# 16-bit slot marks, running sums by a scan, expert tiles spread from step 42 to step 244 with some of them halved, and the last merge divided between VectorE and GpSimd

## What is computed

```python
x = L0_attn_x
xn = _layernorm(x, axis=-1)
x = x + attention(xn, W_q, W_k, W_v, W_o) + experts(xn, Wg, gamma, beta, W1, b1, W2, b2)

# attention: 16 heads of 8 features, rotary embedding, full softmax over 1024 keys
scores = einsum('bhqd,bhkd->bhqk', Q, K) / sqrt(8)
out = einsum('bhqk,bhkd->bhqd', softmax(scores), V) ... @ W_o.T

# experts: 8 experts, each token goes to its best 2
w, idx = top_k(xf @ Wg, 2);  w = softmax(w)
normed = layernorm(xf) * gamma[e] + beta[e]
h = relu(normed @ W1[e] + b1[e])              # 128 -> 512
out = h @ W2[e] + b2[e] + xf                  # 512 -> 128
y = sum over the two chosen experts of w * out
```

## Time and profile before

| | |
|---|---|
| runs (3) | 587.09, 589.49, 590.52 us; median 589.49 |
| profiled execution | 589.15 us, span 587.2 us |
| PE busy | 541.0 us (92%) |
| ACT busy | 501.4 us (85%) |
| DVE busy | 300.9 us (51%) |
| POOL busy | 246.0 us (42%) |
| chain that ended last | PE 63%, ACT 21%, DVE 8% |

### The profile page before, as it was taken

The page is one execution under the profiler, slowest core; times in us unless marked ns, Lnnn a source line. Parts: engine busy times, 40 slices in busy tenths (PEclk is TensorE's granted clock), DMA queues, the critical chain, the costliest instruction groups (busy, mean ns, idle before and its releaser), DMA issues.

```text
span 587.2 us, 12446 instructions
## 1 busy us (share of the span) xinstructions
PE 541.0 (92%) x4620; PEld 246.0 (42%) x4620; DVE 300.9 (51%) x1002; ACT 501.4 (85%) x552; POOL 246.0 (42%) x303
## 2 busy tenths in 40 slices
PE   8899988878999999999899999999989999999783
PEld 6323312222455554445345555434534555554111
DVE  4975789965434344463344433555433444343672
ACT  2699999989898788898888888899899888888992
POOL 4299900078646444556223444365521444322000
PEclk9999999999999999999999999999999999999996
DMA  7144320051435545324443464433433455460821
GB/s 257 29 138 123 113 62 11 1 181 49 159 108 165 185 149 162 99 75 149 136 133 105 163 211 153 141 100 100 160 98 114 154 176 188 142 188 30 315 81 39
DMA packets 44657, 75.47 MB, mean 129 GB/s; under 512 B 7585, under 2 KB 17873, under 8 KB 44081
## 3 DMA queue, kind: packets, MB, share of 16 engines
q1 hardware_dynamic: 39232, 63.71, 33.9%
q0 software_dynamic: 4544, 9.32, 5.2%
q10 hardware_dynamic: 816, 1.61, 0.7%
HBM read 33.88 MB, written 8.85 MB: 73 GB/s over the span
## 4 chain that ended last, share of the span: by engine, by line
PE 63%; ACT 21%; DVE 8%; issue 3%; DMA 2%; POOL 1%; SPq 1%; ACTq 1%; another core or an unknown queue 0%; POOLq 0%; DVEq 0%
PE acc L696 29%; ACT ring L921 20%; PE sc L661 11%; PE aside_bank L740 9%; PE sc L754 8%; PE aside_bank L768 2%; DMA sin<-rope_sin 2%; DVE xn L1228 2%; PE aside_bank L572 1%; PE sc L729 1%; DVE xn L1230 1%; DVE xn L1233 1%; PE aside_bank L588 1%; DVE blocks L1089 1%; SPq L332 1%
## 5 line engine op out<-in xcount | busy, mean ns | idle before, releaser
L921 ACT ACTIVATE ring<-sc 128x1024 f32<-128x1024 f32 x512 | 488.0, 1040 | 59.9 <-PE sc L661 55.9
L696 PE MATMUL acc<-ring,v 128*9 128x512 f32 x2048 | 250.9, 595 | 18.3 <-ACT ring L921 11.8
L513 POOL DMA_INDIRECT work<-normed,token x71 | 71.3, 1004 | 235.1 <-DVE work L1290 181.5
L661 PE MATMUL sc<-qs,ks 32*128 32x512 f16 x1024 | 101.4, 384 | 16.2 <-ACT ring L921 14.1
L1296 DVE TENSOR_SCALAR work<-aside_bank,xn 128x128 f32<-128x128 f32 x216 | 60.8, 345 | 107.1 <-PE aside_bank L740 105.8
L661 PEld LDWEIGHTS sc<-qs,ks 32*128 32x128 f16 x1024 | 26.2, 91 | 177.5 <-ACT ring L921 150.6
L696 PEld LDWEIGHTS acc<-ring,v 128*9 128x9 f32 x2048 | 39.9, 89 | 117.0 <-issue 76.5
L523 POOL DMA_INDIRECT token_out<-work,token x71 | 69.8, 983 | 37.6 <-issue 19.2
L740 PE MATMUL aside_bank<-work,xn 128*128 128x128 f32 x432 | 62.6, 288 | 0.0
L740 PEld LDWEIGHTS aside_bank<-work,xn 128*128 128x128 f32 x432 | 52.3, 191 | 12.2 <-issue 12.2
L754 PE MATMUL sc<-xn,work 128*128 128x128 f32 x432 | 57.2, 275 | 0.0
(11 more groups left out here) (194 smaller groups left out, 416.4 us busy)
## 6 DMA issues: line engine op xcount, KB each, us to landing
xn<-w_rest SPq DMA_DIRECT2D x54, 323.0 KB
xn<-L_ffn_W SPq DMA_DIRECT2D x54, 256.0 KB
w_last<-w_rest SPq DMA_DIRECT2D x17, 323.0 KB
w_last<-L_ffn_W SPq DMA_DIRECT2D x17, 256.0 KB
qs<-hl SPq DMA_DIRECT2D x60, 64.0 KB
ks<-hl SPq DMA_DIRECT2D x60, 64.0 KB
x<-L_attn_x SPq DMA_DIRECT2D x4, 512.0 KB, 8.2
w_rest<-L_ffn_W SPq DMA_DIRECT2D x8, 256.0 KB, 4.0
```

Of the source, the lines that this page charges most:

```text
L513: pool.indirect_dma_start(out=xt[t % TILE_BUFFERS], out_offset=None, in_=xh_d[:, :], in_offset=bass.IndirectOffsetOnAxis(ap=token[:, 0, t: ...
L661: last = nc.tensor.matmul(dst, ks[r:r + 32, kb * P:(kb + 1) * P], qs[r:r + 32, at], start=True, stop=not slow)
L696: last = nc.tensor.matmul(acc[32 * j:32 * j + VW, :], v9[:, b, kb, 4 * g + j, :], ring[:, (2 * n + j // 2) % UNITS, j % 2, :], start=(kb = ...
L921: nc.scalar.activation(ring[:, (2 * n + u) % UNITS, :, :], sc[HOME[2 * n + u]][:, :].rearrange("p (h c) -> p h c", h=2), ACT.Exp, scale=SC ...
```

## The change

1. `mark` compares in 16 bit. Its two index tables are made once by POOL (three copies behind the store of the normed rows), the slots' halves are bf16, and the tables have the 8 columns of a group innermost. `invert` now reads place and name with a step of 8 elements.
2. `place` gets its running sums from two scans instead of chains of shifted additions; `ranks` multiplies by the negated complement of the old triangle.
3. The marks move from steps 32 to 44 to steps 26 to 34, the inversions to 29 to 36, `tokens` from 47 to 36, `owners` to 37, `gates` to 43, the four projections of batch 1 to 38, 40, 46 and 50.
4. The tiles start at step 42 and end at step 242. `ONE_AT` says where layer one of a tile stands, `TWO_AT` where layer two and the turning stand. 58 steps have both. 13 steps have layer one only and 13 others layer two and the turning only, and step 242 the last layer two. `NORM_AT` moves by two steps, and the norm and bound checks share a step with a half.
5. The expert rows are loaded back from step 244 and merged at steps 248 to 251. DVE merges 6 of a batch's 8 rows of tiles (12 instructions instead of 16), POOL the other 2 (4 products and 2 sums a batch). `add_out` of the last batch and the stores wait for both.
6. On PE, `weigh(255)` and `project_out(3, 1)` move into the innermost blocks (`finish`). The last `take_sums`, `divide` and `add_out` of DVE stay behind the blocks.

```diff
-ROUTE_AT, RANKS_AT, SLOTS_AT, OWNER_AT, GATES_AT = 21, 24, 24, 29, 39
-INVERT_AT = {n: g for g, n in enumerate((35, 37, 38, 40, 43, 44, 46, 47))}
-MARK_AT = {n: g for g, n in enumerate((32, 33, 35, 37, 40, 41, 43, 44))}
-TOKENS_AT = 47
-PLAIN_AT = {n: (1, r) for r, n in enumerate((28, 49, 50, 54))}
+ROUTE_AT, RANKS_AT, SLOTS_AT, OWNER_AT, GATES_AT = 21, 24, 24, 37, 43
+INVERT_AT = {n: g for g, n in enumerate(range(29, 29 + GROUPS))}
+MARK_AT = {n: g for g, n in enumerate((26, 27, 29, 30, 31, 32, 33, 34))}
+TOKENS_AT = 36
+PLAIN_AT = {n: (1, r) for r, n in enumerate((38, 40, 46, 50))}
...
-FFN_FROM = 52
-TILE_AT = {n: k for k, n in enumerate([n for n in range(FFN_FROM, STEPS, 2) if n not in TAKEN][:SLOT_TILES + 1])}
+FFN_FROM, FFN_TO = 42, 244
+SMALL = [n for at in (NORM_AT, FLAG_AT) for n in at]
+FREE = [n for n in PAIRS if n not in PLAIN_AT and n not in PROJECT_AT]
+HALVED = [(FREE[FREE.index(n) - 1], n) for n in SMALL]
...
+for n in FREE:
+    if n not in SPLIT_PAIRS or SPLIT_PAIRS.index(n) % 2 == 0:
+        ONE_AT[n] = len(ONE_AT)
+    if n not in SPLIT_PAIRS or SPLIT_PAIRS.index(n) % 2:
+        TWO_AT[n] = len(TWO_AT)
...
-MERGE_AT = {LOAD_AT + 4 + 3 * b: b for b in range(B)}
+LOAD_AT = FFN_TO
+MERGE_AT = {LOAD_AT + 4 + b: b for b in range(B)}
+DVE_TILES = 6
...
+            pool.wait_ge(xh_out, 16 * B)
+            nc.gpsimd.tensor_copy(all_places, iota_p.unsqueeze(2).to_broadcast([P, P, GROUP])).then_inc(indices_ok, 1)
...
+            for b in range(B):
+                pool.wait_ge(y_home[b], 16)
+                y = y_in[b].rearrange("p (t k d) -> p t k d", t=TB, k=2)
+                for k in range(2):
+                    for u in range(DVE_TILES, TB):
+                        t = TB * b + u
+                        last = nc.gpsimd.tensor_scalar(y[:, u, k, :], y[:, u, k, :], small[:, 2 + k, t:t + 1], None, ALU.mult)
+                after(last)
+                rest = x[:, TB * b + DVE_TILES:TB * (b + 1), :]
+                after(nc.gpsimd.tensor_tensor(rest, rest, y[:, DVE_TILES:TB, 0, :], ALU.add))
+                last = nc.gpsimd.tensor_tensor(rest, rest, y[:, DVE_TILES:TB, 1, :], ALU.add)
+                last.then_inc(merged_pool, 1)
...
-                    last = nc.tensor.matmul(bank[0][:, 0:2 * SLOT_TILES], place_mark[g % 2][:, i, :],
-                                            named[g % 2][:, i, :, :].rearrange("p v c -> p (v c)"),
+                    last = nc.tensor.matmul(bank[0][:, 0:2 * SLOT_TILES], place_mark[g % 2][:, :, i],
+                                            named[g % 2][:, :, :, i].rearrange("p v c -> p (v c)"),
...
-                        if n - 2 in TILE_AT:
-                            pe.wait_ge(tile_taken, TILE_AT[n - 2] + 1)
+                        if n - 2 in TWO_AT:
+                            pe.wait_ge(tile_taken, TWO_AT[n - 2] + 1)
...
+            def finish():
+                weigh(STEPS - 1)
+                project_out(B - 1, 1)
...
+                link(nc.vector.tensor_tensor_scan(upto, not_first, totals, 0.0, ALU.mult, ALU.add))
...
+                link(nc.vector.tensor_tensor(tile_mark[k], all_tiles, slot_hl[:, 0, js].unsqueeze(1).to_broadcast(of_tiles),
+                                             ALU.is_equal))
+                nc.vector.tensor_tensor(place_mark[k], all_places,
+                                        slot_hl[:, 1, js].unsqueeze(1).to_broadcast([P, P, GROUP]), ALU.is_equal)
+                nc.vector.tensor_scalar(named[k][:, 0, :, :], tile_mark[k], row_name, None, ALU.mult)
+                nc.vector.tensor_tensor(named[k][:, 1, :, :], tile_mark[k],
+                                        pick_16[:, js].unsqueeze(1).to_broadcast(of_tiles), ALU.mult).then_inc(mark_ok, 1)
...
                 if b == B - 1:
                     v.wait_ge(merged, B)
+                    v.wait_ge(merged_pool, B)
...
-                    for u in range(TB):
+                    for u in range(DVE_TILES):
```

More of the change, by code:

```diff
@@ L98 @@
-SINE_AT = {n + 1 if n != 28 else 48: piece for n, piece in PLAIN_AT.items()}
+FFN_FROM, FFN_TO = 42, 244
+PAIRS = range(FFN_FROM, FFN_TO, 2)
+SMALL = [n for at in (NORM_AT, FLAG_AT) for n in at]
+FREE = [n for n in PAIRS if n not in PLAIN_AT and n not in PROJECT_AT]
+HALVED = [(FREE[FREE.index(n) - 1], n) for n in SMALL]
+SPLIT_PAIRS = [n for pair in HALVED for n in pair]
+MORE = len(FREE) - len(SMALL) - (SLOT_TILES + 1)
+assert len(set(SPLIT_PAIRS)) == 2 * len(SMALL) and MORE >= 0
+for m in range(MORE):
+    at = FREE.index(PER_BATCH + 8 + (STEPS - PER_BATCH) // (MORE + 1) * m)
+    while FREE[at] in SPLIT_PAIRS or FREE[at + 1] in SPLIT_PAIRS:
+        at += 1
+    SPLIT_PAIRS += [FREE[at], FREE[at + 1]]
@@ L99 @@
+ONE_AT, TWO_AT = {}, {}
+for n in FREE:
[3 more added lines that the diff above has]
+        TWO_AT[n] = len(TWO_AT)
+del ONE_AT[max(ONE_AT)]
+TWO_STEP = {k: n for n, k in TWO_AT.items()}
+assert len(ONE_AT) == SLOT_TILES and len(TWO_AT) == SLOT_TILES + 1
+SINE_AT = {n + 1: piece for n, piece in PLAIN_AT.items()}
 SQUARE_AT = {n + 5: piece for n, piece in PLAIN_AT.items() if piece[0] > 1}
-SQUARE_AT.update({n: (1, r) for r, n in enumerate((53, 55, 56, 57))})
@@ L101 @@
-SPLIT_ROUND = {piece: 3 if n < FFN_FROM + 4 else 5 + min(k for k, step in TILE_STEP.items() if step > n)
+SQUARE_AT.update({n: (1, r) for r, n in enumerate((43, 45, 50, 54))})
+SPLIT_ROUND = {piece: 3 if n < FFN_FROM else 5 + max(k for k, step in TWO_STEP.items() if step < n)
                for n, piece in SINE_AT.items()}
-WEIGHTS_AT = {n: k + 3 for n, k in TILE_AT.items() if k >= 1 and k + 3 < SLOT_TILES}
-LOAD_AT = TILE_STEP[SLOT_TILES] + 2
-MERGE_AT = {LOAD_AT + 4 + 3 * b: b for b in range(B)}
+WEIGHTS_AT = {n: k + 3 for n, k in TWO_AT.items() if k >= 1 and k + 3 < SLOT_TILES}
@@ L151, in score_homes @@
             order = [2] + order
-        before = n - 2 if n - 2 in TILE_AT else None
+        before = n - 2 if n - 2 in TWO_AT else None
         for u in range(2):
@@ L671, in maxima @@
                 wait(pe, e_ok, 2 * PER_QUAD * q)
-                wait(pe, tile_taken, len([n for n in TILE_AT if n < PER_QUAD * q]))
+                wait(pe, tile_taken, len([n for n in TWO_AT if n < PER_QUAD * q]))
                 pe.wait_ge(m_wide[b], 2 * (base + 1))
@@ L791, in aside @@
                     first_tile()
-                if n in TILE_AT:
-                    tile(TILE_AT[n], n)
+                if n in ONE_AT:
+                    layer_one(ONE_AT[n])
+                if n in TWO_AT:
+                    layer_two_and_turn(TWO_AT[n], n)
                 if n in NORM_AT:
@@ L854, in batches @@
                         batches(b + 1, following)
+                    else:
+                        finish()
                 with pe.Else():
```

114 lines of the change are left out of this document (49 added, 65 removed).

## The result

The changed kernel takes 607.24 us (median of 4 runs, 606.68 to 607.46); the kernel before took 588.29 us beside it (4 runs, 586.73 to 590.52). The ratio is 1.032, with an interval of 1.028 to 1.036: slower by 3.2%. The forecast was 593.2, with a range of 583.5 to 600, so it was wrong in size. The profiled execution took 607.02 us, of which 605.2 are the span: 18.0 more than the span before.

The account below looks back on a forecast made before the run. Pairs of steps without a tile follow ACT (3.7 us); pairs with one wait over a score home (4.58). Plus 0.3 early, minus 1 tiles, plus 4.6 end is plus 3.9 on 589.15: 593.05, taken as 593.2, range 583.5 to 600.

Parts of the forecast that it names:

- PE's strided reads: Inversions at steps 29 to 36, marks read 16 bytes apart: taken as nothing, bounds nothing to 5.4 us more.
- the case that it matters: Rival of slow marks or inversions: plus 5.4 for doubled strided reads, plus 9 for slow 16-bit comparisons; 598 to 602, chance 0.13.
- The rest of the early part: Steps 24 to 52, marks, inversions, tokens and first tiles: 3.9 us lost where 3.6 were, plus 0.3.
- the row of work: Early marks on DVE 1.75 us each, steps with an inversion on PE 1.9 against ACT's 1.85; both just slower than ACT.
- the wait at step 48: PE's 1.63 us wait before the change, put down to DVE's take_sums being late behind marks and tokens.
- The tiles: Pairs holding layer two or turning cost 4.58 us, others 3.7, wherever tiles stand; halves bring nothing, 1 us less from stalls.
- the prediction's own sign: Pairs with layer two only: under 4.3 us would decide for shorter halves; 4.5 to 4.6 would confirm the forecast.
- halves pay: Rival: a pair's length is PE's own work, so 13 split tiles save 11.4 us, about 582; chance 0.15.
- The minus 1: Stretch of the tiles: 1 us less out of 9.1 of stalls, since PE has slack in 26 more pairs.
- The end: After the last exponential (E): merges take 17.3 us, DVE's branch about 3.0; last sums at E + 8.5, not E + 3.9: plus 4.6.
- The rival of a free end: POOL and DVE don't hinder each other: last sums at E + 2 to E + 4, 587 to 589.5 us; chance 0.25.
- The sum: Whole kernel: plus 0.3, minus 1, plus 4.6 is plus 3.9 on 589.15, so 593.05; taken as 593.2.

Follow-up runs that it names:

- In2_dvefin: in2 with DVE's last take_sums, divide and add_out also moved into the innermost blocks: 594.5 us, ratio 1.007 to the kernel before.
- in2: Changed kernel with 2 of a group's 8 columns innermost in the marks, so PE reads place and names at 4 bytes: 592.03 us, ratio 1.012.
- late: best with marks, tokens and tiles at the steps of the kernel before, owners at step 36: 585.36 us, ratio 0.991.
- B_short2: Kernel before with layer two of each expert tile cut from four matmuls to its first: 587.66 us (1 run).
- best: in2 with whole tiles only, rows loaded back at step 230, all merges on DVE from step 234, both ends inside the blocks: 587.46 us, ratio 0.994.

## Why the prediction was wrong, point by point

- **PE's strided reads: the step that failed.** The prediction named it ("no row shows a strided operand of PE; I take nothing"), set "each read twice as long, 8 x 0.68 = 5.4 more" as its upper bound, and gave the case that it matters 0.13. Measured: 3.3 times as long, 8 x 1.57 = 12.6 us. Both the value and the bound were wrong; the bound was a guess, not a row. The place was seen rightly: PE has no slack at steps 29 to 36, so all of it fell on the path. With the forecast's other terms and 12.6 in place of 0 the sum would be 605.8. The Trainium skill (Advanced Engine Details and Errata, SBUF Cachelines) spoke against the change: accesses that each hit another 16-byte line pay a penalty. The trace agrees in direction; the page gives no size. The page also says that at least two hits on a line are needed to absorb the latency of the access. At a step of 8 bytes there are two, and the matmul still takes 309 ns instead of 225: two hits are not enough here.
- **The rest of the early part.** Forecast plus 0.3. In2_dvefin, which has no slow reads, needs 59.6 us from step 24 to 52: 2.6 for three tiles and 1.6 more than before. In2_dvefin and in2 agree here (59.6 both). So the row of work was sized within 1.3 us: marks 1.73 apart against 1.75, steps of 1.95 with an inversion (87.83 to 89.78 in in2) against 1.9. In the changed kernel 0.7 us are left: 2.3 of more busy time, about what the low clock costs, less the wait of 1.58 that in2 has and the changed kernel has not. By the prediction the wait at step 48 came from marks and `tokens`; late shows that it isn't the marks.
- **The tiles.** Forecast minus 1, with pairs of 4.58 and 3.7 wherever they stand; measured minus 2.4 in the middle stretch and plus 0.3 behind it. B_short2, best and the halves confirm that a pair's length isn't PE's work. The two halves were priced wrongly one by one, 3.7 and 4.58 against 3.99 and 4.27, and rightly in sum (8.28 against 8.26). So the prediction's own sign misleads: it said that a pair with layer two only under 4.3 us would decide for the rival "halves pay". These pairs do take 4.27, and the rival is false all the same, since the pair before them is longer by as much. The minus 1 can't be tested: with this schedule the middle stretch took 405.4 to 412.0 us together with how often ACT started late.
- **The end.** Forecast: last sums 4.6 us later against E. Measured: 5.5 (E + 9.4 against E + 3.9). Merging started at E - 11.8, as forecast; the merges took 17.95 instead of 17.3, DVE's branch 3.13 instead of 3.0. The rival of a free end fell with this.
- **The sum.** Early 14.9, middle minus 2.4, behind it 0.3, tail 5.6, start minus 0.3: 18.1 (18.0 without rounding), against 3.9 forecast. 12.6 of the missing 14.2 are the inversions.

## What to carry to other kernels

Before a layout is turned round for one engine, ask what the other one reads: the streamed operand of a matmul, above all. For the bf16 matmul here it could move 4 bytes from column to column at no cost, and two elements innermost can serve both engines. Where no row shows an operation, a bound taken from "twice" is no bound: it deserves a wide range, and the more so where its engine has no slack. A sign that is to decide between two cases has to be the sum of what the change moves, here two pairs together, and not one of its parts. A busy share near 100% doesn't show that the engine sets the pace; a pair of steps with less work in it, and as long, does.
